# GNN layer and expert FFN on one core: edge steps of three tiles with windows of 32 nodes, four column groups in the fold, and a reordered setup

## The reference, cut to what matters

```python
# x: (1250, 512); 21250 edges sorted by dst (20000 drawn ones and 1250 loops)
def gnn(x, edge_attr, src, dst, ...):
    msg  = relu(x[src] + edge_attr @ W_e + b_e)          # (21250, 512)
    aggr = segment_sum(msg, dst, 1250)
    h = (1 + eps) * x + aggr
    h = silu(batchnorm(h @ W1 + b1, g1, beta1))          # (1250, 1024)
    return silu(batchnorm(h @ W2 + b2, g2, beta2))
x = x + gnn(layernorm(x), ...)
x = x + ffn(layernorm(x))                                # 16 experts, each takes its 156 best tokens
```

## Time and profile before

| | |
|---|---|
| median of three runs | 634.7 us (634.36 to 635.47) |
| the profiled execution | 632.95 us; its span 631.0 us |
| mean granted TensorE clock | 0.905 |
| busy: TensorE, VectorE, ScalarE, GpSimd | 495.0, 392.5, 324.2, 255.9 us |
| setup | 0 to 41 us |
| edge loop | 42 to 300.5 us |

### The profile page before, as it was taken

One profiled execution on the slowest core, in us unless ns is written; L12 is line 12 of the kernel. 1 busy time (PEld: TensorE's weight loads), 2 busy tenths in 40 slices (PEclk: granted clock), 3 DMA queues, 4 the chain that ended last, 5 costly groups with the idle time before them and its releaser, 6 DMA issues.

```text
span 631.0 us, 11762 instructions
## 1 busy us (share of the span) xinstructions
PE 495.0 (78%) x4023; PEld 318.0 (50%) x4023; DVE 392.5 (62%) x961; ACT 324.2 (51%) x660; POOL 255.9 (41%) x245
## 2 busy tenths in 40 slices
PE   1068866799989998998899976811499999999990
PEld 1032221233434333334446535610499999999990
DVE  4747655666666675765579746577747666675530
ACT  2425544555554554554486219534046676675750
POOL 2027777777777765400000000000334655556431
PEclk9977978899999998999999997755589999999995
DMA  9487777777777775611667505740058999984331
GB/s 219 122 276 235 225 220 217 221 227 229 228 230 219 219 220 170 188 43 58 211 220 187 157 0 184 232 178 0 21 152 254 299 278 270 302 234 64 60 41 21
DMA packets 48944, 112.44 MB, mean 178 GB/s; under 512 B 7145, under 2 KB 7565, under 8 KB 48886
## 3 DMA queue, kind: packets, MB, share of 16 engines
q0 software_dynamic: 18992, 54.02, 31.6%
q1 hardware_dynamic: 29399, 57.16, 29.0%
q10 hardware_dynamic: 494, 0.52, 0.4%
HBM read 98.88 MB, written 12.79 MB: 177 GB/s over the span
## 4 chain that ended last, share of the span: by engine, by line
PE 62%; DVE 13%; ACT 10%; issue 6%; DMA 3%; DVEq 3%; POOL 1%; SPq 1%; ACTq 1%; POOLq 0%
PE bank L1333 19%; PE bank L1514 11%; PE bank L1303 10%; PE bank L1324 8%; DVE bank L952 4%; ACT big L599 3%; PE bank L1540 2%; PE bank L1312 2%; DVEq L909 2%; PE bank L1495 2%; PE bank L1504 1%; DVE rows_z L1154 1%; PE bank L1383 1%; DMA big<-in_L_gnn_b_e 1%; ACT rows_z L680 1%
## 5 line engine op out<-in xcount | busy, mean ns | idle before, releaser
L1303 PE MATMUL bank<-big,edge_home 128*64 128x256 f32 x668 | 111.5, 426 | 35.2 <-ACT big L599 35.2
L599 ACT ACTIVATE big<-bank 128x512 f32<-128x512 f32 x167 | 99.5, 596 | 71.7 <-DVE bank L952 68.4
L484 POOL DMA_INDIRECT big<-token_rows,idx x32 | 37.6, 1174 | 221.9 <-DVE idx L1212 214.5
L474 POOL DMA_INDIRECT pair<-node_rows,edge_home x97 | 96.3, 992 | 34.6 <-issue 28.0
L1333 PE MATMUL bank<-big,pair 128*128 128x156 f16 (+2 forms) x1056 | 106.5, 260 | 1.1 <-DVE big L1011 0.9
L1333 PEld LDWEIGHTS bank<-big,pair 128*128 128x128 f16 x1056 | 80.9, 97 | 24.5 <-issue 1.4
L474 POOL DMA_INDIRECT big<-node_rows,edge_home x70 | 67.8, 969 | 62.3 <-DVEq L973 37.9
L1303 PEld LDWEIGHTS bank<-big,edge_home 128*64 128x64 f32 x668 | 35.8, 142 | 93.5 <-issue 58.5
L1324 PE MATMUL bank<-edge_home 64*128 64x512 f16 x501 | 74.0, 403 | 3.4 <-DVE edge_home L926 3.4
L493 POOL DMA_INDIRECT out<-rows_z,idx x32 | 51.0, 1593 | 45.2 <-issue 26.3
L952 DVE TENSOR_TENSOR bank<-pair,bank 128x512 f32<-128x512 f32 x97 | 64.3, 687 | 6.1 <-PE bank L1324 5.3
(11 more groups left out here) (222 smaller groups left out, 778.5 us busy)
## 6 DMA issues: line engine op xcount, KB each, us to landing
raw<-in_L_ffn_w SPq DMA_DIRECT2D x12, 1024.0 KB, 8.5
edge_home<-in_L_ffn_w SPq DMA_DIRECT2D x6, 1024.0 KB, 8.2
pair<-in_L_ffn_w SPq DMA_DIRECT2D x6, 1024.0 KB, 9.7
edge_home<-in_edge_attr SPq DMA_DIRECT2D x19, 320.0 KB, 4.1
xs_home<-in_x SPq DMA_DIRECT2D x10, 448.0 KB
xs_home<-in_L_ffn_w SPq DMA_DIRECT2D x4, 1024.0 KB, 8.2
aggT<-in_L_ffn_w SPq DMA_DIRECT2D x4, 1024.0 KB, 10.6
node_rows<-xs_home SPq DMA_DIRECT2D x5, 448.0 KB
```

The lines of the kernel that those rows point to most:

```text
L474: pool.indirect_dma_start(row(t), None, node_rows, bass.IndirectOffsetOnAxis(src_i[:, t:t + 1], 0)).then_inc(row_in[t % RR], 16)
L484: pool.indirect_dma_start(xg[e % XR][:, a, :], None, token_rows, bass.IndirectOffsetOnAxis(idx[:, e, a:a + 1], 0)).then_inc(xg_in[e % XR], 16)
L599: act.activation(msg[:, t % MR, :], bank[t % PB][0:Q, :], ACT.Relu, scale=1.0 / E_SCALE).then_inc(msg_ready, 1)
L1303: done = pe.matmul(bank[6 + b][a * WIN:(a + 1) * WIN, 0:H // 2], onehot[b][:, j, :], msg[:, t % MR, a * (H // 2):(a + 1) * (H // 2)], star ...
```

## The change

**Sizes.** J goes from 5 to 3 tiles a step (34 to 56 steps) and WIN from 64 to 32 nodes. Edge attributes still come for ten tiles (PAIRS = 5). The step's sum has four feature blocks of 128 in four groups of 32 columns and 32 partitions; it is 128 x 128 and takes one transpose.

**Order in a step.** The transpose stays after the second fold, the accumulate stands after the third (last) add, and its register is loaded ahead of the waits, from a base table that needs no pass index. Part products stand after the first fold; 24 of them go to steps 14 to 46 with gaps; copy and statistics come one step later.

**Setup.** VectorE gives the row and accumulate credits first. Its order by group was statistics 0, scaling of b_e, terms 0, statistics 1, terms 1, table 0, and so on to table 4; it is now statistics 0 and 1, terms 0, statistics 2, terms 1, statistics 3, terms 2, scaling of b_e, table 0, statistics 4, terms 3, table 1, terms 4, tables 2 to 4, and then eps and the node columns. The node transposes use six banks; SP issues the small vectors ahead of its waits for the table.

```diff
-J = 5
+J = 3
+PAIRS = 5
-    WIN = 64
+    WIN = 32
+    FG = 128 // WIN
+    HB = H // FG
-    ZSTEPS = 8
-    ZHEAD = SB - ZPARTS * ZSTEPS
+    SLOPE, OFFSET = 21.5, 14.0
+    ZSTART = (13, 24, 36)
+    ZOFF = (0, 1, 2, 4, 5, 6, 8, 9)
+    ZLAG = 1
+    part_at = {ZSTART[q // F1] + 1 + ZOFF[q % F1]: q for q in range(ZPARTS * F1)}
+    W1_FIRST = ZSTART[0] - 6
+    NB = (0, 1, 2, 5, 6, 7)
...
             load_attr(0)
             sp.dma_start(eps1[:], eps.partition_broadcast(128)).then_inc(params_in, 16)
+            o = 0
+            for v, k in ((b1, F1), (g1, F1), (beta1, F1), (b2, HK), (g2, HK), (beta2, HK)):
+                sp.dma_start(vecA[o:o + k, :], v.rearrange("(k p) -> k p", p=128)).then_inc(vec_in, 16)
+                o += k
+            sp.dma_start(vecB[0:EX * HK, :], fb1.rearrange("e (k p) -> (e k) p", p=128)).then_inc(vec_in, 16)
+            sp.dma_start(vecB[EX * HK:, :], fb2.rearrange("e (k p) -> (e k) p", p=128)).then_inc(vec_in, 16)
+            sp.dma_start(gate_s[:], gate_t).then_inc(vec_in, 16)
...
                 act.activation(aggT[:, :, t * P:(t + 1) * P],
-                               bank[t % 2][:, 0:HK * P].rearrange("p (k n) -> p k n", k=HK),
+                               bank[NB[t % 6]][:, 0:HK * P].rearrange("p (k n) -> p k n", k=HK),
...
-                act.activation(fold_sum[:], bank[6 + i % 2][:, 0:H // 2], ACT.Copy).then_inc(sum_out, 1)
+                act.activation(fold_sum[:], bank[6 + i % 2][:, 0:HB], ACT.Copy).then_inc(sum_out, 1)
...
-                    if j == min(3, last) and i >= ZHEAD:
-                        part_copy(w, i - ZHEAD)
+                    if j == min(0, last) and i - ZLAG in part_at:
+                        part_copy(w, part_at[i - ZLAG])
...
+            def be_scaled():
+                dve.wait_ge(be_in, 32)
+                dve.tensor_scalar(be_all, be_all, E_SCALE, None, ALU.mult).then_inc(be_in, 1)
+
+            dve.sem_inc(row_used, 1)
+            dve.sem_inc(acc_done, 1)
...
             dve.wait_ge(sorted_in, 32)
...
+            statistics(3)
+            norm_terms(2)
+            be_scaled()
...
+            dve.wait_ge(be_in, 33)
             table(0)
+            statistics(4)
+            norm_terms(3)
...
             def accumulate(w, i):
 
+                base = dve.value_load(base_i[0:1, i:i + 1], min_val=0, max_val=N - 1)
                 dve.wait_ge(sum_turned, 1 + w * SB + (i + 1))
                 dve.wait_ge(acc_done, 1 + w * SB + i)
-                base = dve.value_load(base_i[0:1, bass.ds(w * SB + (i + 2), 1)], min_val=0, max_val=N - 1)
                 window = aggT[:, :, bass.ds(base, WIN)]
-                window = window.rearrange("p (a k) n -> p a k n", a=2)
+                window = window.rearrange("p (a k) n -> p a k n", a=FG)
...
+            def bases(w):
+
+                dve.tensor_scalar(shift[:], shift[:], pass_mul[:, bass.ds(w, 1)], pass_add[:, bass.ds(w, 1)],
+                                  ALU.mult, ALU.add).then_inc(based, 1)
+                dve.wait_ge(based, w * 2 + 1)
+                dve.tensor_copy(base_i[:], shift[0:1, :]).then_inc(based, 1)
+                dve.wait_ge(based, w * 2 + 2)
...
-                    if j == min(3, last) and i >= 1:
+                    if j == min(2, last) and i >= 1:
                         accumulate(w, i - 1)
-                    if j == 4 and i % 2 == 0 and i // 2 + 1 < NU:
-                        attr_low(w, i // 2 + 1)
-                if i >= ZHEAD:
-                    part_statistics(w, i - ZHEAD)
+                    if t % (2 * PAIRS) == 4 and t // (2 * PAIRS) + 1 < NU:
+                        attr_low(w, t // (2 * PAIRS) + 1)
+                if i - ZLAG in part_at:
+                    part_statistics(w, part_at[i - ZLAG])
+                if i in ZSTART:
+                    part_low(w, ZSTART.index(i))
...
             def fold(t, j, last, b):
 
-                for a in range(2):
-                    done = pe.matmul(bank[6 + b][a * WIN:(a + 1) * WIN, 0:H // 2], onehot[b][:, j, :],
-                                     msg[:, t % MR, a * (H // 2):(a + 1) * (H // 2)],
+                for a in range(FG):
+                    done = pe.matmul(bank[6 + b][a * WIN:(a + 1) * WIN, 0:HB], onehot[b][:, j, :],
+                                     msg[:, t % MR, a * HB:(a + 1) * HB],
                                      start=(j == 0), stop=(j == last), skip_group_check=True)
...
-                for k in range(HK // 2):
+                for k in range(HB // 128):
                     last = pe.transpose(bank[6 + i % 2][:, k * 128:(k + 1) * 128], fold_sum[:, k * 128:(k + 1) * 128],
                                         ident[:])
...
-                    if j == min(2, last) and i >= ZHEAD:
-                        part_product(w, i - ZHEAD)
+                    if j == min(0, last) and i in part_at:
+                        part_product(w, part_at[i])
```

More of the change, by code:

```diff
@@ L47, in gnn_ffn_kernel @@
     ZPARTS = 3
-    ZSTEPS = 8
-    ZHEAD = SB - ZPARTS * ZSTEPS
+    SLOPE, OFFSET = 21.5, 14.0
+    ZSTART = (13, 24, 36)
+    ZOFF = (0, 1, 2, 4, 5, 6, 8, 9)
+    ZLAG = 1
+    assert all(s * SLOPE - OFFSET >= (c + 1) * ZC for c, s in enumerate(ZSTART))
+    part_at = {ZSTART[q // F1] + 1 + ZOFF[q % F1]: q for q in range(ZPARTS * F1)}
+    assert max(part_at) + ZLAG < SB and all(max(ZOFF) + 1 + ZLAG + s <= z for s, z in zip(ZSTART, ZSTART[1:]))
+    W1_FIRST = ZSTART[0] - 6
     YC = [(0, 250), (250, 375), (625, 625)]
@@ L137, in gnn_ffn_kernel @@
         We16 = edge_take(128, H).bitcast(F16).rearrange("p (w h) -> p w h", w=2)
-        attr16 = [edge_take(2 * ED, J * Q).bitcast(F16).rearrange("p (w n) -> p w n", w=2) for _ in range(2)]
-        attr = [edge_take(2 * ED, J * Q).rearrange("p (c n) -> p c n", c=J) for _ in range(AR)]
+        attr16 = [edge_take(2 * ED, PAIRS * Q).bitcast(F16).rearrange("p (w n) -> p w n", w=2) for _ in range(2)]
+        attr = [edge_take(2 * ED, PAIRS * Q).rearrange("p (c n) -> p c n", c=PAIRS) for _ in range(AR)]
         onehot = [edge_take(Q, J * WIN).rearrange("p (j c) -> p j c", j=J) for _ in range(2)]
@@ L225, in gnn_ffn_kernel @@
         silu = [aggT[:, i, 0:CH[2][1]] for i in range(HK)]
-        half = 2 * J * H
+        half = MR * H
         rows = big[0:Q, 0:half].rearrange("p (s h) -> p s h", h=H)
@@ L236, in row @@
             s = t % RR
-            return rows[:, s, :] if s < 2 * J else late_rows[(s - 2 * J) // 8][:, (s - 2 * J) % 8, :]
+            return rows[:, s, :] if s < MR else late_rows[(s - MR) // 8][:, (s - MR) % 8, :]
         msg = big[0:Q, half:2 * half].rearrange("p (s h) -> p s h", h=H)
@@ L262, in gnn_ffn_kernel @@
             yw.append(rows_z2[0:KH, y0:y0 + 2 * H].rearrange("p (a h) -> p a h", a=2))
-        assert NT == 2 * J and o <= 4 * J * H and y0 + 2 * H <= NT * H
+        assert NT == MR and o <= 2 * MR * H and y0 + 2 * H <= NT * H
         assert 2 * HK * H <= min(edge_words, NT * H, HK * NPAD)
@@ L839, in _ @@
             dve.wait_ge(base_ready, 1)
-            dve.scalar_tensor_tensor(out=early[:], in0=diff[0:SB, 0:1], scalar=33.0, in1=sb_base[:], op0=ALU.mult,
+            dve.scalar_tensor_tensor(out=early[:], in0=diff[0:SB, 0:1], scalar=SLOPE, in1=sb_base[:], op0=ALU.mult,
                                      op1=ALU.add).then_inc(base_ready, 1)
@@ L843, in _ @@
             statistics(0)
-            dve.wait_ge(be_in, 32)
-            dve.tensor_scalar(be_all, be_all, E_SCALE, None, ALU.mult)
             dve.wait_ge(dst_in, 16 * len(LANES_IN))
             dve.tensor_copy(dst_f[:], dst_i[:]).then_inc(base_ready, 1)
+            statistics(1)
             norm_terms(0)
             dve.wait_ge(base_ready, 4)
-            dve.tensor_scalar(early[:], early[:], -14.0, None, ALU.is_lt).then_inc(base_ready, 1)
-            dve.wait_ge(iotas, 9)
+            dve.tensor_scalar(early[:], early[:], -OFFSET, None, ALU.is_lt).then_inc(base_ready, 1)
             dve.wait_ge(base_ps, 1)
-            dve.tensor_copy(base_i[0:1, 2:2 + SB], bank[3][0:1, 0:SB])
             dve.tensor_copy(shift[:, 0:SB], bank[3][0:Q, 0:SB]).then_inc(base_ready, 1)
-            statistics(1)
+            statistics(2)
+            norm_terms(1)
             dve.wait_ge(base_ready, 6)
@@ L886, in _ @@
             dve.memset(aggT[:, :, N:], 0.0)
-            table(4)
+            dve.wait_ge(iotas, 10)
             dve.wait_ge(eps_ready, 1)
@@ L946, in step @@
                 if i == 0:
+                    bases(w)
                     columns_hot(w, 0)
@@ L1276, in node_transposes @@
                 pe.wait_ge(xn_ready, t + 1)
-                if t >= 2:
-                    pe.wait_ge(xt_sb[t % 2], t // 2)
+                if t >= 6:
+                    pe.wait_ge(xt_sb[t % 2], (t - 6) // 2 + 1)
                 for k in range(HK):
-                    last = pe.transpose(bank[t % 2][:, k * P:(k + 1) * P], xn[:, t, k * 128:(k + 1) * 128],
```

(9 more changed lines are left out.)

97 lines of the change are left out of this document (40 added, 57 removed).

## The result

| | before | after |
|---|---|---|
| median of runs | 635.09 us (4 runs, 634.36 to 637.05) | 661.0 us (4 runs, 658.48 to 661.94) |
| ratio to before | 1 | 1.0397, 95% interval 1.0359 to 1.0434 |
| span of the profiled execution | 631.0 us | 659.2 us |
| mean granted clock | 0.905 | 0.867 |

The setup gained and the loop lost more. First the page of after: busy us by engine, and the granted clock in 40 slices.

A forecast was written before the change was run, and what follows sets the result against it. Bound: a round trip through accumulate once a step, not TensorE's work alone. First accumulate 43.5 plus 247.7 plus 24.0 less 0.6 plus 2.5 gives 317.1 against 300.5, 16.6 slower: 651 us, 631 to 670 (612 to 670 with part of the rivals).

The forecast's parts named there:

- the round trip: Edge loop, transpose through accumulate, add, relu, fold and edge products to the next transpose: sets each step, mean 3.84 us plain.
- the walk: Step-by-step timing of setup and loop chain: last accumulate at 317.1 us against 300.5, net 16.6 us slower.
- The start: Setup up to the first add: at 35 us instead of 46.84, a gain of 11.8 us, between 9 and 14.
- the low bound: Setup gain of only 9 us, if the writes, attr and W1 loads slow the first rows by 4 us.
- The fold: TensorE's fold in four column groups: 0.42 us to the next instruction, before 0.59; lower end 0.26, upper 0.59.
- The distances: Between accumulates in the loop: plain steps 3.94 and 3.74 us, part steps 5.52; 30 and 24 of them, 247.7 us.
- The rest of the loop: Splits added to the loop's steps: attr 8.5 us, W1 8, part splits 7.5, together 24.0 us.
- a rival with 0.08: Lower TensorE clock from idling in plain steps: 664 us if a third are hit, 689 if all; chance 0.08.
- The ends: First add to first accumulate 8.5 us, last but one accumulate to last 2.5, no change after the loop.
- The wait at accumulate: VectorE waiting at accumulate for the transposes: some 110 us in all, longest in part steps; before 50.9.
- The ring: Kernel before, edge loop: chain through accumulate closes on itself once a step, 6.1 to 6.3 us for five tiles.
- rival 1: Edge loop: TensorE's work sets the pace, so the change gives 603 us, or 620 half way; chance 0.27.

The follow-up runs named there:

- e1: Changed kernel with only the part products moved, from behind the first fold to behind the same step's transpose; 626.47 us, ratio 0.9857 to the kernel before.
- e2: Changed kernel with accumulate moved behind the next step's first add and part splits one step later; 594.25 us, ratio 0.9353 to the kernel before.
- f4: Changed kernel with accumulate's register load put behind its waits again; 717.33 us, ratio 1.1302 to the kernel before.
- g1: Changed kernel, part products behind the transpose and accumulate behind the next first add, W1 loads held until table written and eighth row landed; 589.55 us.
- f3: Changed kernel with twelve unused matmuls of constants ahead of each step's first fold, filling TensorE's waits; 642.2 us, ratio 1.0118 to the kernel before.
- f2: Kernel before (five tiles, windows of 64, old setup) with accumulate behind the next step's first add, one sum late; 631.79 us, ratio 0.9963.
- g3: Kernel before (five tiles, windows of 64) with new setup, later accumulate, and part products' copy and statistics one step later; 597.68 us, ratio 0.9428.
- e3: Changed kernel with part products behind the transpose and accumulate behind the next step's first add; 589.4 us, ratio 0.9297 to the kernel before.

## Why the prediction was right, and where it was short

The direction, the mechanism and its place were right: the round trip, now taken 56 times, with the part product on it (e1, e2 and f4 each move it alone). The size was 16 us against 26. By its steps, on the spans (16.6 foretold, 28.2 measured; that no more is missing is in part luck, since the walk was 14 us too long where the rest of the loop was 22 too short):

- **The start**, 11.8 us earlier: 8.7, just under its bounds. VectorE's order, the node copies and the first edge product came within 0.4 us of the walk; the gathers began 3 us later than assumed and the first row took 6.4 us instead of 5.0, so that the rows were not hidden. The reason given for the low bound, slow first rows, is borne out by g1: without the W1 loads beside it the first row takes 3.7 us.
- **The fold**, 0.42 us: 0.36 (246.17 to 246.53), between the upper end of 0.59 and the lower of 0.26. The Trainium skill (TensorEngine Tiling (Array Packing), "Theoretical Speedup") states up to 4x for a dimension of 32. The estimate that the prediction made by it is 0.31; the measured 0.36 lies between that and the 0.42 from the pace of the earlier trace rows.
- **The distances**: plain 3.94 and 3.74 foretold, 3.75 and 3.58 at full clock; part steps 5.52, measured 5.31 and 4.99. At these measured values 30 plain and 24 part steps come to 30 x 3.665 + 24 x 5.15 = 233.6 us, 14 below the walk.
- **The rest of the loop**, 24 us for attr, W1 and part splits: the 54 distances sum to 279.6, so 46.0. This is the mis-sized term, and what it lacks is the lower clock. In f3, at nearly full clock, the 54 distances sum to 260.7, which by the same step values leaves 27, near the 24; so the clock is some 17 to 19 of the 22 us missing. The prediction kept it apart as a rival with 0.08 and looked for it in plain steps. It came mostly in part and splitting steps; the few plain steps at granted 0.50 took 5.14 us (from 93.06) and 4.83 (from 298.02), 1.4 and 1.25 more, near the 1.3 that the rival had.
- **The ends**: the first accumulate came 7.2 us after the first add (8.5 foretold), the last two are 0.9 apart (2.5), and the stage after the loop, which I had at no change and any change of which I had named a sign of being wrong, took 2.8 us more. Of these 1.7 are L1377's 32 matmuls (L1399 now), which start at the lower clock there (granted 0.50 from 326 to 330 us): 438 ns each in the mean instead of 374.
- **The wait at accumulate**, some 110 us: 120.3.
- **What bounds before**: half right. The ring was there, but f2 shows that with five tiles the stall on the statistics stood close behind it, and g3 that both must go. That TensorE's work sets the pace (rival 1) is refuted for the changed kernel by e1; three tiles or five, it was the order.

## What to carry to other kernels

A smaller step takes its round trip more often; before cutting steps, walk the ring through the in-order engines once, and count what stands on it and not only what each engine has to do. Here two moves in the order were worth 72 us, against 18 for the narrow folds, and a wait on the ring cost more than its length, as the clock fell more often (f4: 56 us for 39). When a wait is removed, look at what is second latest: with five tiles the same move gained 3 us alone and, with the statistics' lag and the new setup, 37.

## What the runs showed of the hardware

Four column groups of 32 columns side by side took 0.36 us for eight records of 128 columns in float32, where two groups of 64 took 0.59 for four records of 256. The granted clock fell in steps in which TensorE stood 1.75 us and was otherwise busy (0.76 over 188 to 195 us), and held at 1.00 through the same wait at 246.17 (1.00 over 240 to 260 us); what decides between them is not shown. Some 0.84 us of filling matmuls per step raised it (0.86 to 0.98 over the loop, f3). A register load, with its queue instructions, put behind a wait on VectorE cost 0.72 us a step (f4). The first gather's rows came 6.3 us after its start with the W1 loads beside it (e3) and 3.7 us after it without them (g1).
